# One load of the logarithm and exponential tables, scatter indices read from the row, twelve w_lo pieces on the Pool engine

## What is computed

```python
x = _layernorm(x + _L0_attn_ref(x, W_qkv, b_qkv, W_out, b_out))       # softmax(q k^T) v W_out
# _L0_ffn_ref:
h = x + layer_norm(x, ln1_g, ln1_b) @ attn_w.T
t = layer_norm(h, ln2_g, ln2_b).reshape(-1, H)
top_vals, top_idx = top_k(t @ gate_w.T, 2)
rw = softmax(top_vals)
for e in range(8):
    out += comb[:, e:e + 1] * ((silu(t @ gate_proj[e].T) * (t @ up_proj[e].T)) @ down_proj[e].T)
x = _layernorm(x + h + out)
```

## Time and profile before

| | us |
|---|---|
| runs, median of three | 474.45 (473.22 to 474.63) |
| the profiled execution's own time | 471.38 |
| span of its trace | 469.5 |
| front, up to the first load of `xrow` | 0 to 188.8 |
| experts, up to the start of the last scatter | 188.8 to 428.6 |
| finish | 428.6 to 469.5 |

### The profile page before, as it was taken

One profiled execution on the slowest core, in us unless ns is written; L12 is line 12 of the kernel. 1 busy time (PEld: TensorE's weight loads), 2 busy tenths in 40 slices (PEclk: granted clock), 3 DMA queues, 4 the chain that ended last, 5 costly groups with the idle time before them and its releaser, 6 DMA issues.

```text
span 469.5 us, 9229 instructions
## 1 busy us (share of the span) xinstructions
PE 323.4 (69%) x1968; PEld 271.6 (58%) x1969; DVE 282.2 (60%) x1091; ACT 224.8 (48%) x485; POOL 196.5 (42%) x307
## 2 busy tenths in 40 slices
PE   5764674854942510699999999999999999991000
PEld 4654564753842410488877777877777777781000
DVE  3566475665666563378765656566565565660993
ACT  3877759669578550244433333343333343430353
POOL 0001242633624537134444444454444454434893
PEclk9987978879777555599999999999999999996555
DMA  8711302302206223111111111111111111102671
GB/s 245 285 47 35 113 25 68 92 19 74 68 31 211 94 66 99 29 41 41 48 34 45 34 45 29 45 35 42 45 34 45 31 33 43 38 29 65 187 238 57
DMA packets 35467, 33.85 MB, mean 72 GB/s; under 512 B 4833, under 2 KB 31845, under 8 KB 35312
## 3 DMA queue, kind: packets, MB, share of 16 engines
q1 hardware_dynamic: 26192, 22.65, 16.8%
q0 software_dynamic: 4320, 8.53, 5.1%
q10 hardware_dynamic: 4928, 2.37, 1.7%
HBM read 20.19 MB, written 11.68 MB: 68 GB/s over the span
## 4 chain that ended last, share of the span: by engine, by line
DMA 40%; issue 15%; PE 15%; DVE 11%; ACT 10%; POOL 5%; POOLq 2%; SPq 1%; ACTq 0%; DVEq 0%
DMA moe_rows<-ysb,idx 34%; DMA w_raw<-weights 3%; POOL idx L1064 3%; PE bank L438 3%; PE bank L505 3%; PE bank_pair L475 2%; ACT L619 2%; ACT L656 2%; POOL expert_rows L1045 2%; ACT prob L646 1%; DVE xs L1004 1%; POOLq L1073 1%; DVE mv L1013 1%; PE bank L453 1%; PE bank L462 1%
## 5 line engine op out<-in xcount | busy, mean ns | idle before, releaser
L1045 POOL DMA_INDIRECT expert_rows<-rows,place x64 | 63.7, 995 | 122.1 <-DVE rows L902 98.6
L1068 POOL DMA_INDIRECT moe_rows<-ysb,idx x71 | 70.5, 992 | 32.0 <-issue 32.0
L562 PE MATMUL bank_pair<-wd,hidT 128*128 x568 | 77.1, 279 | 0.7 <-ACT ysb L688 0.6
L973 DVE TENSOR_SCALAR tn<-xrow 128x128 f32<-128x128 f32 x71 | 25.0, 352 | 82.6 <-DMA xrow<-expert_rows 82.4
L562 PEld LDWEIGHTS bank_pair<-wd,hidT 128*128 128x128 f32 x568 | 68.9, 192 | 2.8 <-issue 1.7
L688 ACT ACTIVATE ysb<-bank_pair 128x128 f32<-128x128 f32 x71 | 19.7, 277 | 104.7 <-PE bank_pair L562 104.7
L523 PE MATMUL bank<-w_hi,t_hi 128*128 x142 | 64.1, 451 | 8.1 <-DVE t_lo L982 6.5
L682 ACT ACTIVATE prob<-bank 128x512 f32<-128x512 f32 x71 | 42.5, 598 | 35.1 <-PE bank L525 34.9
L1064 POOL TENSOR_TENSOR idx<-xrow,zero_i 128x1 int32<-128x1 int32 x71 | 15.2, 214 | 102.4 <-DMA moe_rows<-ysb,idx 87.6
L990 DVE SCALAR_TENSOR_TENSOR probT<-prob,xrow,bank 128x512 f32<-128x512 f32 x71 | 52.7, 743 | 7.7 <-PE bank L525 6.1
L525 PE MATMUL bank<-w_hi,t_lo 128*128 x142 | 57.0, 401 | 0.0
(11 more groups left out here) (161 smaller groups left out, 617.9 us busy)
## 6 DMA issues: line engine op xcount, KB each, us to landing
xrow<-expert_rows SPq DMA_DIRECT2D x71, 66.0 KB, 1.9
w_raw<-weights SPq DMA_DIRECT2D x16, 256.0 KB, 4.5
w_raw<-moe_rows SPq DMA_DIRECT2D x16, 256.0 KB, 3.7
wd<-weights SPq DMA_DIRECT2D x1, 2048.0 KB, 9.6
out<-xs ACTq DMA_DIRECT2D x16, 128.0 KB, 3.1
rows<-rows SPq DMA_DIRECT2D x7, 258.0 KB, 2.8
xT<-xt SPq DMA_DIRECT2D x3, 512.0 KB, 5.4
xs<-x SPq DMA_DIRECT2D x3, 512.0 KB, 5.3
```

Source lines behind the costliest of these rows:

```text
L562: last = mm(banks[7][:, 0:P], hidT[i2][:, c * P:(c + 1) * P], wd[:, bass.ds(w + c * P, P)], start=(c == 0), stop=(c == NC - 1))
L1045: G.indirect_dma_start(out=expert_rows[:, :], out_offset=bass.IndirectOffsetOnAxis(ap=place[:, i, k:k + 1], axis=0), in_=rows[:, i, k, :], ...
L1068: G.indirect_dma_start(out=moe_rows[:, :], out_offset=bass.IndirectOffsetOnAxis(ap=idx[r4][:, :], axis=0), in_=ysb[r4][:, :], in_offset=No ...
```

## The change

Four edits.

- ACT starts with one explicit load of a table set that holds logarithm and exponential both. The one load for silu ahead of the experts stays.
- `PIECES` becomes three pieces in each of the steps 0 to 3 and one in each of the steps 7, 9, 11 and 13. The subtraction that gives `w_lo` is done by POOL for the first twelve pieces, ahead of its first scatter, and by DVE for the last four. SP's loads into `w_raw` wait for POOL's subtractions.
- `idx` and its instruction are gone. The scatter of a result reads the row numbers straight from the destination column of `xrow`, which now has eight buffers. SP's load of tile s waits for `tn` of tile s-4 and for the scatter of tile s-8.
- In POOL's step the part of the residual now comes ahead of the scatter. `hidT` uses the memory of `nT`, which only the front needs; this pays for the buffers.

```diff
+            nc.scalar.add_instruction(mybir.InstLoadActFuncSet(name=nc.get_next_instruction_name(),
+                                                               act_func_set_id=LN_EXP_TABLES))
...
-        xrow = ring("xrow", [P, ROW], n=RING)
+        xrow = ring("xrow", [P, ROW], n=XR)
...
-        hidT = ring("hidT", [P, INTER])
+        hidT = nT
...
-        PIECES = [2, 2, 2, 2, 1, 1, 0, 1, 0, 1, 0, 1, 0, 1, 0, 1, 0, 1]
+        PIECES = [3, 3, 3, 3, 0, 0, 0, 1, 0, 1, 0, 1, 0, 1]
+        BY_POOL = 12
...
                 for i in pieces(s):
                     if i >= NWR:
-                        sp.wait_ge(sm["wlo_done"], i - NWR + 1)
+                        j = i - NWR
+                        sp.wait_ge(sm["wlo_pool"], j + 1) if j < BY_POOL else sp.wait_ge(sm["wlo_done"], j + 1 - BY_POOL)
...
             def load_rows(s, r, live):
                 if live(0):
+                    r4 = r % RING
+                    at = sp.value_load(rowoff[0:1, bass.ds(s, 1)], min_val=0, max_val=X_ROWS - P)
                     if far(s, RING):
-                        sp.wait_ge(sm["hid_done"], s - (RING - 1))
-                        sp.wait_ge(sm["idx_done"], s - (RING - 1))
-                    at = sp.value_load(rowoff[0:1, bass.ds(s, 1)], min_val=0, max_val=X_ROWS - P)
-                    sp.dma_start(xrow[r][:, :], expert_rows[bass.ds(at, P), :]).then_inc(xr_in[r], 16)
+                        sp.wait_ge(sm["tn_done"], s - (RING - 1))
+                    if far(s, XR):
+                        sp.wait_ge(y_sent[r4], turn(s - XR, r4))
+                    sp.dma_start(xrow[r][:, :], expert_rows[bass.ds(at, P), :]).then_inc(xr_in[r4], 16)
...
+            for i in range(BY_POOL):
+                pool.wait_ge(sm["whi_done"], i + 1)
+                cs = slice(i * WP, (i + 1) * WP)
+                G.tensor_tensor(w_lo[:, :, cs], w_raw[i % NWR][:, :, :], w_hi[:, :, cs].bitcast(F32),
+                                ALU.subtract).then_inc(sm["wlo_pool"], 1)
...
             def experts(s, r, live):
                 if live(4):
-                    pool.wait_ge(sm["idx_done"], s - 3)
+                    r4 = r % RING
                     pool.wait_ge(sm["ysb_done"], s - 3)
-                if live(1):
-                    i, r1 = s - 1, (r - 1) % RING
-                    pool.wait_ge(xr_in[r1], turn(i, r1))
-                    if far(i, RING):
-                        pool.wait_ge(y_sent[r1], turn(i, r1) - 16)
-                    G.tensor_tensor(idx[r1][:, :], xrow[r1][:, C_DST:C_DST + 1].bitcast(I32), zero_i[:, :], ALU.add
-                                    ).then_inc(sm["idx_done"], 1)
```

More of the change, by code:

```diff
@@ L32 @@
 RES = D // 2
+LN_EXP_TABLES = 6
 GROUPS = [[0]] + [[b, b + 1] for b in range(1, B - 1, 2)] + [[B - 1]]
@@ L82 @@
 NV = 3
+XR = 8
 def block_kernel(nc, x, xt, par, con, dst, weights, out):
@@ L200, in block_kernel @@
         hid = [a[:, :, :].rearrange("p t k -> p (t k)") for a in probT]
-        hidT = ring("hidT", [P, INTER])
+        hidT = nT
         warm = sb("warm", [P, 1])
-        zero_i = sb("zero_i", [P, 1], I32)
-        idx = ring("idx", [P, 1], I32, n=RING)
         ysb = ring("ysb", [P, D], n=RING)
@@ L257, in block_kernel @@
                  "cnt_done dn_done dnt_done eidx_done past_done "
-                 "ereg_done row_done plan_done warm_done fill_ready fill_done odd_filled whi_done wlo_done "
+                 "ereg_done row_done plan_done warm_done fill_ready fill_done odd_filled whi_done wlo_done wlo_pool "
                  "tn_done xr_ps t32_done thi_done tlo_done g_ps u_ps sg_done hid_done hT_ps hT_sb y_ps ysb_done "
-                 "zero_ready idx_done "
                  "z0_done z_done st3_done mv3_done var3_done rs3_done shift3_done o_done").split()
@@ L284, in looped_steps @@
             for s in range(first):
-                step(s, s % RING, lambda lag, s=s: 0 <= s - lag < n_items)
+                step(s, s % UNROLL, lambda lag, s=s: 0 <= s - lag < n_items)
             with eng.Fori(0, turns) as i:
                 for r in range(UNROLL):
-                    step(i * UNROLL + (first + r), r % RING, lambda lag: True)
+                    step(i * UNROLL + (first + r), (first + r) % UNROLL, lambda lag: True)
             for s in range(first + UNROLL * turns, n_items + depth):
-                step(s, s % RING, lambda lag, s=s: 0 <= s - lag < n_items)
+                step(s, s % UNROLL, lambda lag, s=s: 0 <= s - lag < n_items)
         def far(i, n):
@@ L509, in _ @@
             straight_steps(front, B, FRONT)
-            pe.wait_ge(sm["wlo_done"], B)
+            pe.wait_ge(sm["wlo_pool"], BY_POOL)
+            pe.wait_ge(sm["wlo_done"], B - BY_POOL)
             pe.wait_ge(sm["wd_in"], 16)
@@ L916, in front @@
                 for i in pieces(s):
+                    if i < BY_POOL:
+                        continue
                     dve.wait_ge(sm["whi_done"], i + 1)
@@ L969, in experts @@
                 if live(0):
-                    dve.wait_ge(xr_in[r], turn(s, r))
+                    dve.wait_ge(xr_in[r % RING], turn(s, r % RING))
                     if far(s, 2):
@@ L984, in experts @@
                 if live(2):
-                    i, i2, r2 = s - 2, r % 2, (r - 2) % RING
+                    i, i2, r2 = s - 2, r % 2, (r - 2) % XR
                     dve.wait_ge(sm["sg_done"], i + 1)
@@ L1031, in _ @@
             G = nc.gpsimd
-            G.memset(zero_i[:, :], 0).then_inc(sm["zero_ready"], 1)
-            pool.wait_ge(sm["zero_ready"], 1)
+            for i in range(BY_POOL):
[3 more added lines that the diff above has]
+                                ALU.subtract).then_inc(sm["wlo_pool"], 1)
             pool.wait_ge(sm["half_ready"], 1)
@@ L1056, in experts @@
                 if live(4):
-                    pool.wait_ge(sm["idx_done"], s - 3)
+                    r4 = r % RING
                     pool.wait_ge(sm["ysb_done"], s - 3)
-                if live(1):
-                    i, r1 = s - 1, (r - 1) % RING
-                    pool.wait_ge(xr_in[r1], turn(i, r1))
-                    if far(i, RING):
-                        pool.wait_ge(y_sent[r1], turn(i, r1) - 16)
-                    G.tensor_tensor(idx[r1][:, :], xrow[r1][:, C_DST:C_DST + 1].bitcast(I32), zero_i[:, :], ALU.add
-                                    ).then_inc(sm["idx_done"], 1)
-                if live(4):
-                    r4 = r % RING
-                    G.indirect_dma_start(
-                        out=moe_rows[:, :], out_offset=bass.IndirectOffsetOnAxis(ap=idx[r4][:, :], axis=0),
-                        in_=ysb[r4][:, :], in_offset=None, bounds_check=last_row, oob_is_err=False
-                    ).then_inc(y_sent[r4], 16)
                 if not isinstance(s, int) or s < 2 * TOKEN_TILES:
@@ L1075, in experts @@
                                     ).then_inc(sm["res_done"], 1)
+                if live(4):
+                    G.indirect_dma_start(
+                        out=moe_rows[:, :],
+                        out_offset=bass.IndirectOffsetOnAxis(ap=xrow[(r - 4) % XR][:, C_DST:C_DST + 1].bitcast(I32), axis=0),
+                        in_=ysb[r4][:, :], in_offset=None, bounds_check=last_row, oob_is_err=False
+                    ).then_inc(y_sent[r4], 16)
             looped_steps(pool, experts, MOE_TILES, 4)
```

## The result

The changed kernel takes 403.1 us (402.4 to 403.8, four runs) where the kernel before took 473.8 beside it: a ratio of 0.851, with a 95% interval of 0.848 to 0.854. The forecast was 405.7, in a range of 400 to 417. The profiled execution is 402.85 us long with a span of 401.0, and the working summed to 402.6 for it; the forecast for the median then added the 3.1 us by which the profiled execution of the kernel before had been shorter than its median, and here that difference is 0.25 us.

A forecast was written before the change was run, and what follows sets the result against it. Bounds: in the experts POOL's wait for each scatter's landing, in the front a dependency chain through all engines. Terms -1 + 4.4 + 27.0 + 4.7 + 4.7 + 29.0 = 68.8 us took 474.45 to 405.7, range 400 to 417.

The forecast's parts named there:

- The pair without loads, 5 x 3.8: Front, five pairs of steps ending in 7 to 15: without table loads each pair loses 3.8 us.
- The clock, 5 x 1.6: Front, same five pairs: PE's wait shortens to 2.2 us, its clock stays full, 1.6 us gained a pair.
- the rival in which the clock still falls: Front: PE's clock falls in each shorter wait, losing 9.6 us, 415; chance 0.22 shared with DVE being held off.
- The start, -1 and +4.4: Front's first steps: twelve pieces in steps 0 to 3 lose 1 us; the pair of steps 4 and 5 gains 4.4.
- Steps 16 and 17: Late front pair: 3.1 us from table loads plus 1.6 us from the clock, 4.7 us gained.
- the end of the front: After the last attention matmul: 2.1 us from no late piece and 2.6 from table loads, 4.7 us gained.
- POOL holds DVE off: Start and experts: POOL's work delays DVE through shared ports, 10 us, 416; chance 0.22 shared with the clock falling.
- The experts, 25.8 + 3.2: Experts: tiles at PE's pace of 2.846 us gain 25.8 us; the last scatter following its product sooner gains 3.2.
- the rival in which the experts stay above it: Experts: a tile takes 3.07 us instead of 2.85, costing 15 us, 420; chance 0.07.
- the one in which table loads stay in the front: Front: the explicit load does not hold, only 29 us of gain remain, 446; chance 0.01.
- The slower rival, the ring of eight: Experts: SP's load waits for the scatter eight tiles back; slower than before, above 475, if landing takes 12 us; chance 0.01.
- The term of 2.1 us for the last `w_lo`: Front's end: DVE turns late to attention's result, after a piece loaded behind `wd`; no piece there gains 2.1 us.

## Why the prediction came out right, point by point

**The pair without loads, 5 x 3.8.** Right. PE's wait went from 6.02 to 2.12 us, 3.9 less, and its transposes are what is late next.

**The clock, 5 x 1.6.** Right in kind, wrong in the pattern, and one of the prediction's own signs of being wrong, 0.50 in the clock's row in mid-front, came true. The forecast took one level for all waits of 2.2 us, from one row; two of the five pairs still ran on at half the clock. The pairs gained 5.5, 4.0, 6.0, 4.1 and 6.0, in all 25.6 of 27.0. So the rival in which the clock still falls is true for two pairs, and the run with dummies shows its price, 1.3 us a pair, not the 1.6 taken. One row of a short wait with its clock kept did not carry the claim for five. How many pairs run at half the clock is no fixed number either (three and four of five in two runs with one front): with four, the changed kernel would have taken some 2.6 us more, by an estimate of 2 x 1.3.

**The start, -1 and +4.4.** Step 3's seed ends 1.2 us sooner, not 1 later, and by step 5 4.6 are gained of 3.4. That may be chance: in the four other traces with these first steps the second seed of step 5 ends at 36.20 to 37.84, 2.8 to 4.4 us sooner than the 40.60 of the kernel before. `w_hi` ended step 3 at 28.13, forecast 28.4; but the seed stands ahead of step 3's pieces, and only 9 of 12 were before it. Steps 16 and 17 gave 3.5 of 4.7, the end of the front 4.1 of 4.7.

**POOL holds DVE off.** It does, once at nearly full size. POOL's twelve subtractions took 1.27 us each (1.2 taken). DVE beside the first of them, and beside the three of step 2:

```profile
11.32 0.86 DVE L912 COPY rows<-dests 128x64 int32<-128x64 int32 x1
...
20.41 3.73 POOL L1043 TENSOR_TENSOR w_lo<-w_raw,w_hi 128x512 fp32r<-128x512 f32 x3 [1.52 <-ACT w_hi L656]
...
22.70 0.23 DVE L817 SCALAR_TENSOR_TENSOR half<-v,seed 128x4 f32<-128x4 f32 x1 [2.18 <-ACT seed L627]
22.96 1.19 DVE L820 TENSOR_TENSOR corr<-half,seed 128x4 f32<-128x4 f32 x1
...
24.98 0.88 ACT L638 ACTIVATE xs<-xs,shift,r 128x128 f32<-128x128 f32 x2 [1.31 <-DVE shift L836]
```

An instruction that takes 0.16 to 0.17 us elsewhere took 1.19 until POOL was through, and ACT waited for it. It ended at 24.15, POOL's third subtraction at 24.13. L817 just ahead of it took 0.23, for it started when the second subtraction had only 0.21 us left, and ended 0.02 behind it. L912, a copy that takes 0.22 in the kernel before, took 0.86 and ended at 12.18, 0.08 behind the first subtraction. The other DVE instructions beside the twelve, none with two inputs in SBUF, took what they take elsewhere; a copy of one column (L917) is among them. The four other traces with these first steps agree: L817 took 0.34 to 0.96 us in them and ended 0.02 behind a subtraction each time. The rule cited ahead (the Trainium skill, SBUF — State Buffer, section SBUF: two separate sides) now has its row for a 128x512 operation. The rival's 10 us did not come, for in the experts `t_hi` takes 0.279 us on average where it took 0.229 before (49 of its 71 ended 0.09 behind the residual's instruction), and in front of it DVE waits 24.9 us in all for ACT: there is room for it.

**The experts, 25.8 + 3.2.** Right: a tile takes 2.83 us (2.846 taken), the last scatter follows its product by 1.74 us (1.9). Of the 1.7 us more than forecast, 58 x 0.019 = 1.1 are the pace (2.827 us in the mean). The runs with the scatter's edit alone and with eight `idx` buffers show that the wait for a landing was what held the pace above PE's. So the rival in which the experts stay above it did not come, nor did the one in which table loads stay in the front: two are left in all.

**The slower rival, the ring of eight.** Its mechanism is real and its price far larger than any other (1041 us with four buffers), its point of decision is 1.5 to 3.0 us away. The forecast's slack was "some 5 us". One of the signs in "what would show it wrong", SP waiting for `y_sent`, came true 62 times and meant nothing: SP runs ahead and waits at each buffer; the sign to read is DVE's wait for `xrow`, 0.4 us in all.

**The sum.** The terms were added as if independent. The three parts alone give 31.4, 30.2 and 0.1 us, 61.7 together, and the whole 70.7. The term of 2.1 us for the last `w_lo` belongs to the pieces and exists only while a piece stands behind `wd`; its size grows to 4.9 and 5.8 us when the loads go. The forecast had both edits in its working at once, so the sum came out; as prices of single edits its terms would have misled.

## What to carry to other kernels

Look first at what one engine alternates between: two small functions from two table sets cost 5.1 us a pair of steps here, and one explicit load removed it; and don't let a producer wait for the landing of what it has just issued when a deeper ring is to be had. Price an edit together with the others, since work that hides behind a stall becomes the stall when that goes. A wait of PE can cost twice, itself and the clock after it; dummy matmuls inside the wait, which end just before it does, buy the second part back. And compare kernels on one chip: the same front took 27 us longer on another.

## What the runs showed of the hardware

- Two waits of PE of 2.12 us, with the same work around them, left the clock at 1.00 once and halved it the next time, at a price of 1.3 us in the pair; and one front ran three of five pairs at half the clock in one execution and four in another. Twelve matmuls of 128x256 in bf16, 1.47 us, kept it at 1.00 throughout.
- The 36 loads of a table set cost their own 1.28 us each and nothing visible beside it, and with one load ahead a logarithm and its exponential take 0.47 us from start to end (100.60 to 101.07).
- A scatter that reads its row numbers from one column of a wider buffer takes 0.995 us to issue, as one from a buffer of its own does (0.99).
- Beside POOL's subtraction of 128x512 a DVE instruction of 128x4 with two inputs in SBUF, and a copy of 128x64, took until that subtraction ended: 1.19 us in place of 0.17, and 0.86 in place of 0.22.
- On one chip DVE and ACT waited 2.5 to 5.7 us in up to five steps of the front for something that the trace puts to no engine, when PE's rows that they wait for had long ended; five kernels out of five have it there, and a front of the same code on another chip has not. Left open.
